# A graph network's two gather passes: degree products, roots, join and key tables moved to the tails, group 0 added ahead of own one-hots

## The reference, cut to what matters

```python
# layer 0, edge network
h = x
for _ in range(2):
    m_ij = relu(concat([h[ei], h[ej], edge_attr]) @ We1 + be1) @ We2 + be2
    h = h + segment_sum(m_ij, ej)
x = layernorm(x + h + bias)
# layer 1, graph convolution (loops of weight 1 added)
deg  = segment_sum(ew, dst)
dinv = where(deg > 0, rsqrt(where(deg > 0, deg, 1)), 0)
norm = dinv[src] * ew * dinv[dst]
out  = segment_sum((x @ weight.T)[src] * norm, dst) + bias1
x = layernorm(x + relu(out) + x)
```

## Time and profile before

| | us |
|---|---|
| runs | 2446.34, 2449.79, 5570.81 (median 2449.79) |
| the profiled execution | 2445.97 |
| its span | 2443.8 |
| PE busy | 2198.1 (90%) |
| POOL busy | 1698.7 (70%) |
| DVE busy | 1396.8 (57%) |
| ACT busy | 894.8 (37%) |
| mean granted clock of PE | 0.936 of full |

### The profile page before, as it was taken

The page is one execution under the profiler, slowest core; times in us unless marked ns, Lnnn a source line. Parts: engine busy times, 40 slices in busy tenths (PEclk is TensorE's granted clock), DMA queues, the critical chain, the costliest instruction groups (busy, mean ns, idle before and its releaser), DMA issues.

```text
span 2443.8 us, 49886 instructions
## 1 busy us (share of the span) xinstructions
PE 2198.1 (90%) x14876; PEld 1725.2 (71%) x15066; DVE 1396.8 (57%) x3830; ACT 894.8 (37%) x1461; POOL 1698.7 (70%) x1765
## 2 busy tenths in 40 slices
PE   2799999999999997899999999899998779999996
PEld 2577666676667666666666666666666679999995
DVE  1755555555555552464555555555543477787775
ACT  1533344434443432233343444344433332222322
POOL 1677777777777776267777777777777467677673
PEclk8899999999999995699999999999998579999998
DMA  5333333333333333333333333333333221121111
GB/s 122 97 102 101 102 101 101 101 102 102 101 102 102 102 101 92 93 87 97 102 102 100 102 100 102 100 100 101 102 101 99 57 63 50 48 52 50 48 48 49
DMA packets 156484, 218.67 MB, mean 89 GB/s; under 512 B 74232, under 2 KB 107887, under 8 KB 156276
## 3 DMA queue, kind: packets, MB, share of 16 engines
q0 software_dynamic: 56000, 114.80, 18.3%
q1 hardware_dynamic: 93236, 98.88, 14.6%
q10 hardware_dynamic: 7168, 4.09, 0.6%
HBM read 207.48 MB, written 10.12 MB: 89 GB/s over the span
## 4 chain that ended last, share of the span: by engine, by line
POOL 46%; issue 29%; PE 17%; DMA 3%; DVE 3%; ACT 1%; POOLq 1%; SPq 0%; DVEq 0%
POOL gat L524 46%; PE ps L709 5%; PE ps L718 5%; PE ps L595 3%; DMA gat<-p_dram,idx 1%; DMA gat<-dst_row 1%; PE ps L792 1%; DMA cbase_dram<-cint 1%; DMA gat<-z_dram,idx 1%; PE ps L788 1%; PE ps L618 1%; PE ps L658 0%; PE ps L634 0%; DVE node_a L1207 0%; DVE msg L1226 0%
## 5 line engine op out<-in xcount | busy, mean ns | idle before, releaser
L524 POOL DMA_INDIRECT gat<-p_dram,idx x1422 | 1367.8, 962 | 512.8 <-issue 430.4
L658 PE MATMUL ps<-node_a,x 128*128 128x512 bf16 x2210 | 683.2, 384 | 11.8 <-issue 2.4
L1226 DVE TENSOR_TENSOR msg<-ps,gat 128x512 f32<-128x512 f32 (+1 forms) x404 | 252.9, 627 | 685.7 <-DMA gat<-p_dram,idx 598.8
L595 PE MATMUL ps<-hot,msg 128*128 128x64 f32 x3232 | 447.2, 287 | 100.4 <-ACT msg L910 86.6
L1207 DVE TENSOR_SCALAR node_a<-ps,row_id 128x512 bf16<-128x512 f16 x1200 | 486.5, 475 | 46.2 <-PE ps L641 36.5
L595 PEld LDWEIGHTS ps<-hot,msg 128*128 128x128 f32 x3232 | 408.4, 200 | 128.8 <-ACT msg L910 107.3
L658 PE MATMUL ps<-node_a,adj 128*128 128x512 bf16 x1200 | 460.1, 383 | 0.0
L584 PEld LDWEIGHTS ps<-rhs,lhs 96*128 96x128 f32 x3232 | 408.7, 199 | 54.1 <-ACT lhs L891 25.3
L584 PE MATMUL ps<-rhs,lhs 96*128 96x128 f32 x3232 | 412.6, 283 | 24.7 <-ACT lhs L891 17.2
L524 POOL DMA_INDIRECT gat<-z_dram,idx x328 | 320.9, 978 | 158.7 <-issue 100.4
L658 PEld LDWEIGHTS ps<-node_a,x 128*128 128x128 bf16 x2400 | 238.4, 103 | 245.5 <-issue 12.6
(11 more groups left out here) (147 smaller groups left out, 1787.5 us busy)
## 6 DMA issues: line engine op xcount, KB each, us to landing
dbc<-dst_row SPq DMA_DIRECT2D x202, 256.0 KB
lhs<-eaT SPq DMA_DIRECT2D x202, 128.0 KB
gat<-p_dram,idx POOLq DMA_INDIRECT x1422
rhs<-q_dram SPq DMA_DIRECT2D x202, 32.0 KB
gat<-z_dram,idx POOLq DMA_INDIRECT x328
idx<-src_g SPq DMA_DIRECT2D x243, 4.0 KB
p_dram<-node_a ACTq DMA_DIRECT2D x12, 256.0 KB, 3.3
q_dram<-node_b SPq DMA_DIRECT2D x12, 256.0 KB, 3.4
```

What stands on the lines that cost most here:

```text
L524: return pool.indirect_dma_start(out=out_, out_offset=None, in_=table, in_offset=bass.IndirectOffsetOnAxis(ap=index, axis=0))
L595: last = nc.tensor.matmul(ps_agg(s), (msg if p < 2 else gat)[s][:, c, :], hot[s][:, c, (0 if p < 2 else 1), :], start=(c == 0), stop=(c == ...
L658: mm = nc.tensor.matmul(ps_own, p_part[k][:, t, :], shot[j % 2][:, t - t0, :, :].rearrange("p j e -> p (j e)"), start=(t == 0 and k == 0), ...
L1226: V.tensor_tensor(msg[s][:, c0:c1, :], ps_pre(s, h)[:, 0:(c1 - c0) * P].rearrange("p (c f) -> p c f", f=P), gat[s][:, c0:c1, :], ALU.add). ...
```

## The change

Five things move, and nothing is computed differently:

1. In both passes, step 0 of DVE makes group 0's additions and group 1's one-hots ahead of own one-hots 2 (they stood behind).
2. The keys of pass 0 are made in two parts after steps 96 and 97, in place of after step 1.
3. The degree products are made on PE after the sums of group 94 of pass 1, DVE's four operations on them after step 95, ACT's root after step 96.
4. The join and the end of `dinv` come on DVE after step 97 of pass 1, in place of after step 1.
5. In pass 1, ACT makes group 0's one-hots between its two cuts of the table, in place of after both.

With the degree products gone, PE, ACT and DVE have no wait on them at the head of pass 1.

```diff
+DEG_AT = 4 * BATCHES - 2          # 94
@@ PE
-                if p == 1:
-                    for t in range(TILES):
-                        mm = nc.tensor.matmul(ps[:, 7, t:t + 1], cw[:, t * P:(t + 1) * P], parts[:, 0:1],
-                                              start=True, stop=True)
-                    mm.then_inc(deg_mm, 1)
+                def degree_products():
+                    for t in range(TILES):
+                        mm = nc.tensor.matmul(ps_deg[:, t:t + 1], cw[:, t * P:(t + 1) * P], parts[:, 0:1],
+                                              start=True, stop=True)
+                    mm.then_inc(deg_mm, 1)
...
                         sums(g, s)
+                        if p == 1 and type(g) is int and g == DEG_AT:
+                            degree_products()
...
                         if p == 0:
                             pe.wait_ge(ids_kept, 2)
-                        else:
-                            pe.wait_ge(dchain, 1)
                         turn_ids(0)
@@ ACT
-                    else:
+                    def degree_roots():
                         act.wait_ge(dchain, 3)
                         nc.scalar.activation(dtmp[:, :], dtmp[:, :], ACT.Sqrt).then_inc(ln_std, 1)
...
                             nc.scalar.activation(m, m, ACT.Relu).then_inc(relu_done, 1)
+                            if p == 1 and type(g) is int and g == DEG_AT + 2:
+                                degree_roots()
...
+                        if p == 1:
+                            one_hots(0, 0, 1)
                         for q, (t0, n) in enumerate(QUADS):
                             n = min(n, HI - t0)
                             act.wait_ge(part_left, 2 * len(QUADS) * p + q + 1)
                             nc.scalar.copy(p_part[1][:, t0:t0 + n, :], rest[:, t0:t0 + n, :]).then_inc(part_cut, 1)
-                        act.wait_ge(rel_ready, 2)
-                        one_hots(0, 0, 1)
+                        if p == 0:
+                            act.wait_ge(rel_ready, 2)
+                            one_hots(0, 0, 1)
@@ DVE
-                        dve.wait_ge(deg_mm, 1)
...
                         dve.wait_ge(agg_clear, 2)
+                def degrees():
+                    dve.wait_ge(deg_mm, 1)
...
-                        if q is not None and j < 3:
+                        first = type(g) is int and g == 0
+                        if first:
+                            pass
+                        elif q is not None and j < 3:
                             own_hots(j + 1, q)
...
                             scatter_hots(g + 1, 1 - s)
-                        if type(g) is int and g == 1:
-                            (chunk_keys if p == 0 else join)()
+                        if first:
+                            own_hots(j + 1, q)
+                        if p == 0 and type(g) is int and g == DEG_AT + 2:
+                            chunk_lanes()
+                        if p == 0 and type(g) is int and g == DEG_AT + 3:
+                            chunk_columns()
+                        if p == 1 and type(g) is int and g == DEG_AT + 1:
+                            degrees()
+                        if p == 1 and type(g) is int and g == DEG_AT + 3:
+                            join()
```

More of the change, by code:

```diff
@@ L195, in build @@
         ps_own = ps[:, 6, :]
+        ps_deg = ps[:, 7, 0:TILES]
         ps_ids = ps[:, 7, :].bitcast(f16)[:, 0:4 * P]
@@ L1148, in _ @@
                     else:
-                        dve.wait_ge(deg_mm, 1)
-                        V.tensor_scalar_add(deg[:, :], ps[:, 7, 0:TILES], 1.0).then_inc(dchain, 1)
-                        dve.wait_ge(dchain, 1)
-                        V.tensor_single_scalar(dmask[:, :], deg[:, :], 0.0, ALU.is_gt).then_inc(dchain, 1)
-                        dve.wait_ge(dchain, 2)
-                        V.tensor_copy(dtmp[:, :], ones[:, 0:1].to_broadcast([P, TILES])).then_inc(bounds, 1)
-                        dve.wait_ge(bounds, 14)
-                        V.copy_predicated(dtmp[:, :], dmask[:, :].bitcast(mybir.dt.uint32), deg[:, :]
-                                          ).then_inc(dchain, 1)
-                        dve.wait_ge(agg_clear, 2)
+                        dve.wait_ge(agg_clear, 2)
+                def degrees():
+                    dve.wait_ge(deg_mm, 1)
+                    V.tensor_scalar_add(deg[:, :], ps_deg, 1.0).then_inc(dchain, 1)
+                    dve.wait_ge(dchain, 1)
+                    V.tensor_single_scalar(dmask[:, :], deg[:, :], 0.0, ALU.is_gt).then_inc(dchain, 1)
+                    dve.wait_ge(dchain, 2)
+                    V.tensor_copy(dtmp[:, :], ones[:, 0:1].to_broadcast([P, TILES])).then_inc(bounds, 1)
+                    dve.wait_ge(bounds, 14)
+                    V.copy_predicated(dtmp[:, :], dmask[:, :].bitcast(mybir.dt.uint32), deg[:, :]
+                                      ).then_inc(dchain, 1)
                 with dve.If(fast == 1):
@@ L1324, in _ @@
                     if p == 1:
+                        degrees()
                         join()
                     if p == 0:
-                        chunk_keys()
+                        chunk_lanes()
+                        chunk_columns()
                         V.memset(lhs[0][0:W, :], 0.0).then_inc(g_group, 1)
```

6 lines of the change are left out of this document (5 added, 1 removed).

## The result

The changed kernel takes 2440.13 us (median of 6 runs, 2438.38 to 2442.13 but for one disturbed run) against 2447.41 us: ratio 0.9969 (one disturbed run on each side left out), 95% interval 0.9958 to 0.9981, about 7.5 us faster. Two further comparisons of the same pair gave 0.9959 (0.9945 to 0.9974) and 0.9960 (0.9945 to 0.9975), about 10 us. The forecast was 13.7 us. So the class (within 2%) and the range of 2425 to 2444 held, and of the gain about a third is missing over the three comparisons, nearly half in this first one.

What follows compares the result with a forecast made beforehand. POOL's serial gathers were taken to bound passes 0 and 1, PE close behind. Gains of 3.4 us (pass 0) and 10.3 (pass 1), 13.7 off 2445.97, gave 2432.3; forecast put at 2434 for run scatter, range 2425 to 2444.

Steps and rivals of the forecast that it cites:

- Mid pass: After the head of pass 0, PE's slack is gained batch by batch; no further stall, so no loss.
- Part 1, pass 0: Head of pass 0: group 0's earlier addition restarts POOL 6.4 us sooner; group 4 waits for turned ids, gain 4.2 us.
- Part 2: Key tables moved from head to tail of pass 0: tail pays 0 to 1.6 us, taken as 0.8.
- Part 3: Head of pass 1: POOL's 11.48 us pause goes whole; group 4 comes 13.6 us earlier (12 to 15.1).
- Part 4: Join moved to the tail of pass 1: holds a gather there, costing 2.4 to 3.3 us, taken as 3.3.
- Part 5: Degree products in the tail of pass 1: PE late by up to 11.2 us but catches up; cost 0, at most 1.
- A: Rival: PE limits neither head, POOL's group 4 comes at its own pace; 17.4 us gained, 2430; chance 0.20.
- B: Rival: low clock holds for both first own parts of pass 1, 7.8 us late; 7.6 gained in all, 2440; chance 0.18.
- C: Rival: PE, not POOL, sets the pass; between nothing and 5 us slower, 2451 with products at 8.9; chance 0.10.

Runs made afterwards that it cites:

- short one-hots: Target one-hots and their pass 0 cast cover one chunk of 8 from group 3 on: changed kernel so edited 2418.18 us (0.9881), kernel before so edited 2427.05 us (0.9923).
- edit to columns: Changed kernel with each set of target one-hots made by 8 one-chunk operations, one SBUF tensor and a scalar column each: 2414.47 us, ratio 0.9868.

## Why the prediction was right or wrong

**Mid pass.** "Afterwards the PE slack is gained batch by batch, so I expect no further stall" is the step that failed. No stall by a wait came, as the two kernels with short one-hots show, but the gathers themselves became longer: 2.8 us in pass 0. The rows of before had it (3 to 10 us of excess over the step of the earlier trace rows); I read POOL's waits, and a gather that is held counts there as busy. By stretches, the sum that I put down was 4.2 - 0.8 + 13.6 - 3.3 = 13.7 us; the traces have 3.5 - 0.9 + 10.6 - 2.4, less 2.8 in mid pass 0, less 0.2 between the passes and plus 0.3 in mid pass 1: 8.1. The range was wide enough to hold this; it was not drawn for the loss in mid pass. What fixes the excess of pass 0 could be narrowed, not settled. Of its 28 gathers in a batch, the 18th loses 3.1 to 3.3 us in all in the five kernels with the key tables in the tail (and the one-hot in one piece), and 0.6 to 1.1 us in the five with them at the head. There the cast begins 0.17 us before the gather in the changed kernel, and 0.28 us in the other:

```profile
398.64 0.41 DVE L1093 CAST hot<-hot 128x512 bf16<-128x512 f32 x1
```

```profile
398.81 1.05 POOL L526 DMA_INDIRECT gat<-p_dram,idx  x1 [0.30 <-issue]
```

```profile
399.52 0.41 DVE L1093 CAST hot<-hot 128x512 bf16<-128x512 f32 x1
```

```profile
399.80 0.95 POOL L526 DMA_INDIRECT gat<-p_dram,idx  x1 [0.30 <-issue]
```

The cast ends 0.24 us into the first gather and 0.13 into the second, and each gather ends 0.81 to 0.82 us after its cast; a cast that ends less than some 0.13 us into a gather costs it nothing. Why tables made at the end of the pass move the phase of the batches ahead of them stays open.

**Part 1, pass 0: right.** The pause is 5.58 and 3.33 us, foretold as 5 to 6 and 3 to 4; the gain 3.5 us, foretold as 4.2.

**Part 2: right in size, wrong in sign of the choice.** The tail paid 0.9 us (0.8 foretold). But at the head the tables had cost nothing that POOL didn't wait for anyway, and the place in the tail costs the excess of mid pass besides: 3 us for nothing.

**Part 3: right in kind, too large by 3 us.** 10.6 us in place of 13.6. The pause went whole. The two traces can be set side by side as they stand, for PE's table products begin at 1000.50 and 1000.70. PE's first own part began at 1031.94 and not at 1029.6, by four mis-sized terms. The products L620 took 14.25 us in place of 13.33, in

```profile
1000.70 13.33 PE L618 MATMUL ps<-wpq,hT 128*128 128x128 f32 x104
```

of the kernel before, so everything behind them came 0.8 us later (in this trace; over all traces the stretch between the passes is 0.2 us longer). DVE's rest began at 1019.80 and not at 1018.8. The row of targets landed some 5.4 us after its issue, where I had taken 3.5 to 5, and ACT's second cut held DVE's third part 1.20 us. PE began 2.90 us after the own one-hots did (1029.04), where I had counted 2.4. From there to the turn it took 1052.62 - 1031.94 = 20.7 us, foretold as 18.8 + 1.7: the loss to the low clock was right. The turn to group 4 took 4.24 us, as foretold (4.2). Then came a term that the forecast lacked: group 4's second gather starts 3.01 us after its first in all traces of the changed kernel, 1.76 more than usual. DVE is not the cause: the first gather is held by a one-hot (1.36 us), but with short one-hots or columns it takes 0.94 and the second still starts 3.01 us after it. The trace shows one transfer of instructions on a queue of its own (q14) between 1055 and 1056 us, just ahead of it; in the kernel before one lies ahead of group 4 without a pause. That it is the loading of POOL's code was not tested.

**Part 4: right, below its number.** The tail paid 2.4 us in the changed kernel (3.4 in the pair with short one-hots), foretold as 3.3 with 2.4 as the lower end. The loss follows the phase, but not as I wrote it: it is smaller where the join is partly done when the gather begins, and the gathers that began first were not held. The gather began 1.21 us after the join here and 0.29 us before, and ends 0.82 after it either way. I had weighed a rule of the Trainium skill (SBUF — State Buffer, Who interferes with whom), that two SBUF inputs meet only GpSimd's reads and that descriptor writing is inferred to be free. That a gather pays nothing beside such an operation, as I drew from it, does not hold here: with the join moved away the 2.2 us came back. A gather also reads its row numbers from SBUF (`idx`), so its rule on reads could cover this, and no run here separates the two. The same section's rule that a DVE operation with at most one SBUF input, outside of the two-port modes, does not contend agrees with the additions, which take their other input from PSUM and held none of 653 gathers. Its rule that a cast and a `tensor_scalar` can enter such a mode agrees with the casts and the columns, which hold gathers.

**Part 5: right.** The products of degrees took 8.75 us on PE and cost nothing:

```profile
1869.87 8.75 PE L636 MATMUL ps<-parts,cw 4*128 4x1 f32 x52
...
1890.52 3.78 PE L586 MATMUL ps<-rhs,lhs 96*128 96x128 f32 x16 [2.11 <-ACT lhs L898]
...
1922.82 1.94 PE L597 MATMUL ps<-hot,msg 128*128 128x64 f32 x8 [3.48 <-ACT msg L912]
```

PE had idle again at 1890.5, not at 1927 as I had worked out at the lower clock all through: one group in between took 2.00 us for its products (at 1884.44) in place of 3.78, and the sums on both sides of it 2.06 and 1.90.

**The rivals.** A (PE is no limiter, 17.4 us) fell: POOL waited for the turn in both passes. B's number, 7.6 us, is nearly what came, by another way: one low stretch of some 4.5 us cost 2 us, and the second own part ran at the full clock. C fell: no pause of more than 0.32 us in mid pass, in any trace, and PE followed a POOL that was quicker still.

## What to carry to other kernels

When a wait of the leading engine is removed, list what holds its own instructions too: an instruction that is held by another engine's operation shows as busy and in no list of waits, and only the distances of its starts, or the count of them in a window, tell. Where POOL issues gathers back to back, keep long VectorE operations with all their inputs in SBUF (casts too) out of its way: put them where POOL waits or rests anyway, or, as here with one SBUF tensor and a scalar column, write them as several short ones, even if that takes VectorE twice as long. And before moving work away from a head, ask whether the leading engine stands at a later gate there: what is hidden behind that gate is free at its old place, and isn't at the new one.

## What was not expected of the hardware

A gather that begins while VectorE runs an operation with two SBUF inputs ends 0.81 to 0.83 us after that operation, at every length seen: 0.69 us (1.40 for the gather), 1.00 (1.54), 3.68 (3.29 and 4.21); one operation of the key tables gave 0.86, and a short one (L1083, 0.35 us) held none of the 11 gathers that began 0.05 to 0.06 us after it. If the gather began first, or less than 0.045 us after, it was not held in mid pass 1. Casts and `tensor_scalar` columns within SBUF hold gathers too; additions and comparisons with an input from PSUM do not. A column of 0.25 us cost a gather at most 0.14 us where one operation of 0.69 cost it some 0.45. The edit to columns is worth 22 us here, of which 11 us in mid pass are accounted for by this; that is more than the whole change under study.
